# Gated cross-attention and a two-expert feed-forward: the sorted rows packed without a gap

## The reference

```
x = x + tanh(g_xattn) * attention(layernorm(x), ctx)      # 16 heads of 16, 77 keys, softmax, output projection
n = layernorm(x)                                          # 2048 rows of 256
top1 = argmax(n @ gate_w.T)                               # expert 0 or 1 for each row
masked[e] = n where top1 == e, else 0
routed = sum over e of relu(masked[e] @ w1[e] + b1[e]) @ w2[e] + b2[e]      # hidden 1024
shared = relu(n @ sw1 + sb1) @ sw2 + sb2
x = x + tanh(g_ffn) * (routed + shared)
```

## Time and profile before

| | us |
|---|---|
| median of 3 runs (lowest, highest) | 352.51 (351.61, 352.97) |
| the profiled execution | 354.73 |
| its span | 353.0 |
| PE busy in the span | 323.2 (92%) |
| DVE busy | 223.5 (63%) |
| ACT busy | 217.3 (62%) |
| POOL busy | 197.1 (56%) |

### The profile page before, as it was taken

How to read it: one execution, slowest core, us unless ns; L and a number is a source line. 1 busy time by engine, 2 the same in 40 slices (tenths; PEclk the granted TensorE clock), 3 DMA queues, 4 the chain that set the end, 5 groups by cost and what they waited for, 6 DMA issues and landing times.

```text
span 353.0 us, 7375 instructions
## 1 busy us (share of the span) xinstructions
PE 323.2 (92%) x2407; PEld 288.8 (82%) x2407; DVE 223.5 (63%) x490; ACT 217.3 (62%) x491; POOL 197.1 (56%) x274
## 2 busy tenths in 40 slices
PE   7984769889999999999999989999999999999970
PEld 6662658667989778797889969999999999999970
DVE  6999578999889657668957925334354435343540
ACT  3565586976785866847948553546655656464640
POOL 7467578673765478537480785244553544464432
PEclk9999588999999999999999999999999999999996
DMA  6999695280515241203330210212311321022110
GB/s 193 293 308 240 107 315 146 71 212 4 143 34 120 43 92 58 72 3 120 121 119 2 68 53 30 88 34 63 89 60 30 89 78 37 25 71 88 49 41 30
DMA packets 40230, 33.88 MB, mean 96 GB/s; under 512 B 16697, under 2 KB 37709, under 8 KB 40205
## 3 DMA queue, kind: packets, MB, share of 16 engines
q1 hardware_dynamic: 36552, 25.80, 27.2%
q0 software_dynamic: 2816, 7.09, 6.3%
q10 hardware_dynamic: 837, 0.67, 0.7%
HBM read 21.72 MB, written 12.35 MB: 97 GB/s over the span
## 4 chain that ended last, share of the span: by engine, by line
PE 67%; DVE 10%; DMA 6%; POOL 5%; SPq 4%; issue 3%; ACT 1%; another core or an unknown queue 1%; ACTq 0%; POOLq 0%; DVEq 0%
PE y_ps L1405 23%; PE h_ps L1405 16%; PE s_ps L1405 11%; PE bank L1405 10%; DMA x_all<-in_x 5%; PE bank L1538 4%; SPq L516 1%; DVE smax L1173 1%; POOL sorted_dram L667 1%; PE bank L1642 1%; DVE rsum L1191 1%; SPq L458 1%; DMA k_own<-k_dram 1%; POOL hT_lo L676 1%; POOL nt L692 1%
## 5 line engine op out<-in xcount | busy, mean ns | idle before, releaser
L1371 DVE TENSOR_TENSOR hT_lo<-h,hT_hi 128x256 fp32r<-128x256 f32 x72 | 32.5, 452 | 45.2 <-ACT h L1027 42.1
L648 POOL TENSOR_TENSOR probs<-probs,rinv 128x616 f32<-128x616 f32 x32 | 41.4, 1293 | 27.6 <-DVE rinv L1195 27.5
L1024 ACT ACTIVATE hT_hi<-h_ps,vec_cols 128x256 fp32r<-128x256 f32 x36 | 17.1, 475 | 43.3 <-PE h_ps L1405 39.9
L1405 PE MATMUL y_ps<-ew_hi,hT_hi 128*128 128x256 f32 x144 | 41.5, 288 | 0.0
L1405 PE MATMUL y_ps<-ew_hi,hT_lo 128*128 128x256 f32 x144 | 40.3, 280 | 0.0
L1405 PE MATMUL y_ps<-ew_lo,hT_hi 128*128 128x256 f32 x144 | 40.3, 280 | 0.0
L937 ACT ACTIVATE hT_hi<-h_ps,vec_cols 128x512 fp32r<-128x512 f32 (+1 forms) x40 | 24.7, 617 | 24.8 <-PE h_ps L1405 24.4
L1405 PE MATMUL y_ps<-sw_hi,hT_hi 128*128 128x256 f32 x128 | 38.1, 297 | 1.8 <-POOL hT_lo L676 1.7
L777 POOL DMA_INDIRECT out<-final,scatter_token x18 | 19.6, 1092 | 29.9 <-issue 16.2
L1405 PE MATMUL y_ps<-sw_lo,hT_hi 128*128 128x256 f32 x128 | 36.1, 282 | 0.0
L1405 PE MATMUL y_ps<-sw_hi,hT_lo 128*128 128x256 f32 x128 | 36.1, 282 | 0.0
(11 more groups left out here) (197 smaller groups left out, 1054.8 us busy)
## 6 DMA issues: line engine op xcount, KB each, us to landing
v_diag<-v_rows SPq DMA_DIRECT2D x16, 256.0 KB
stage<-in_L_ffn_w SPq DMA_DIRECT2D x4, 1024.0 KB, 5.4
sorted_dram<-empty_rows SPq DMA_DIRECT2D x10, 257.0 KB, 8.9
xs<-sorted_dram SPq DMA_DIRECT2D x10, 257.0 KB
stage<-in_L_ffn_sw SPq DMA_DIRECT2D x2, 1024.0 KB, 7.1
x_all<-in_x SPq DMA_DIRECT2D x1, 1536.0 KB, 10.3
part_dram<-x_all SPq DMA_DIRECT2D x3, 512.0 KB
k_dram<-probs SPq DMA_DIRECT2D x2, 616.0 KB, 10.2
```

Source lines behind the costliest of these rows:

```text
L648: nc.gpsimd.tensor_tensor(pq, pq, rinv[:, b % 2, k, :].unsqueeze(2).to_broadcast([P, HG, KEYS]), ALU.mult).then_inc(p_ready, 1)
L1024: nc.scalar.activation(hT[0][:, c % HB, 0:RTOK], hidden_bank(c % 4)[:, 0:RTOK], ACT.Relu, bias=b1_sb[:, 1 + e, c:c + 1]).then_inc(h_hi, 1)
L1371: nc.vector.tensor_tensor(hT[1][:, c % HB, 0:RTOK], h32[:, c % 2, 0:RTOK], hT[0][:, c % HB, 0:RTOK], ALU.subtract).then_inc(h_lo, 1)
L1405: return nc.tensor.matmul(out_, lhsT, rhs, start=start, stop=stop, **kw)
```

## The change

The rows are packed without a gap: rows of expert 0 from the front, rows of expert 1 from the back of exactly 2048 slots. The tile in the middle then has rows of both. It is run with one expert only, the one that has the middle of the tile, and the half of it (128 rows) in which the seam lies is run again at the end with the other expert, and only the rows of that expert are written. So there are 8 rounds (9 if one expert has at most 128 rows) and a half tile.

- One fill DMA is left, of the 256 slots behind the end.
- `seam` computes five numbers (`plan`) in seven more small DVE operations, and three for the rows to be dropped.
- Into the place of the shared weights, ACT copies the weights of the half tile's expert by four DMAs of 1 MB each from SBUF to SBUF, after its waits for the last shared product and all expert weights and before its first routed evacuation.
- The half tile: first layer of 8 x 2 x 3 products with 128 columns, second layer of 8 x 3 products with 256 columns; evacuations and splits of 128 columns; one gather, one add, one final of 256 columns and one scatter.
- All five orders are new. POOL splits chunks 1, 4 and 5 of a unit instead of 1, 3, 4, 5 and 6; ten quarters are folded instead of eleven.

```diff
-RTILES = TOKENS // RTOK + 1
-SLOTS = RTILES * RTOK
+RTILES = TOKENS // RTOK
+MOST_ROUNDS = RTILES + 1
-LO_ON_POOL = (1, 3, 4, 5, 6)
-FOLDED = {2, 4, 11, 12, 16, 19, 22, 23, 26, 28, 31}
+LO_ON_POOL = (1, 4, 5)
+FOLDED = {2, 4, 11, 12, 16, 19, 25, 29, 30, 31}
...
 PE_ORDER = """
-    warm.0 yt.0 yt.1 yt.2 yt.3 vt warm.1 kp.0.0 kp.0.1 in.0.0 kp.1.0 kp.1.1 qy.0.1 vp.0 in.1.0 vp.1 vp.2 qy.1.1
-    sc.0.0 sc.0.1 vp.3 sc.0.2 sc.0.3 sc.1.0 sc.1.1 in.2.0 tn.0.0.1 tn.0.1.1 qy.2.0 sc.1.2 sc.1.3 tn.0.2.1
+    warm.0 yt.0 yt.1 yt.2 yt.3 vt warm.1 kp.0.0 in.0.0 kp.0.1 kp.1.0 qy.0.1 kp.1.1 sc.0.0 vp.0 in.1.0 vp.1 vp.2
+    qy.1.1 vp.3 sc.0.1 sc.0.2 sc.0.3 sc.1.0 sc.1.1 tn.0.0.0 tn.0.1.1 in.2.0 qy.2.1 sc.1.2 sc.1.3 tn.0.2.0
...
-    di.7.3 hl.19 hl.20 ro.3.0 ro.3.1 hl.21 ro.3.2 ro.3.3 hl.22 ro.4.0 ro.4.1 scat.3 hl.25 ro.4.2 ro.4.3 hl.27
-    hl.28 hl.29 scat.4 hl.30 hl.33 hl.35 hl.36 hl.37 hl.38
+    ro.2.0 ro.2.1 ro.2.2 ro.2.3 di.6.2 scat.1 di.6.3 di.7.0 scat.2 hl.17 di.7.1 di.7.2 di.7.3 hl.20 hl.21 ro.3.0
+    ro.3.1 ro.3.2 ro.3.3 hl.25 ro.4.0 ro.4.1 hl.28 ro.4.2 hl.29 ro.4.3 scat.3 scat.4 hl.33 hl.36 hl.37
...
 SP_ORDER = """
-    fl.0 fl.1 kw.0 vz.0 vz.1 kw.1 fl.2 fl.3 kr.1 kr.2 vw.0 fl.4 vw.1 wd.0 wd.1 vr.0 kr.3 vw.2 vr.1 wd.3 kr.4
-    vr.2 vw.3 wd.2 vw.4 kr.5 vr.3 vr.4 vw.5 kr.6 vr.5 vw.6 ps.0 vw.7 kr.7 vr.6 vr.7 ps.1 wd.4 wd.5 ps.2 xs ps.3
-    ps.4
+    fl.0 kw.0 vz.0 vz.1 kw.1 kr.1 kr.2 wd.0 vw.0 wd.1 vw.1 vr.0 kr.3 vw.2 vr.1 vr.2 kr.4 vw.3 wd.3 vw.4 vr.3
+    kr.5 vr.4 wd.2 vw.5 vw.6 vr.5 kr.6 vw.7 ps.0 kr.7 vr.6 vr.7 ps.1 wd.4 wd.5 ps.2 ps.3 xs ps.4
 """
...
@@ SP
+            def fill():
 
                 sp.wait_ge(empty_made, 2)
+                rows = sorted_dram[TOKENS:TOKENS + RTOK, :].rearrange("(t p) d -> p t d", p=P)
+                sp.dma_start(rows, empty_rows[:, :, :]).then_inc(filled, 16)
...
+            with sp.Fori(0, rounds - 1) as j:
                 sp.wait_ge(xsT_ps, j + 1)
                 sp.wait_ge(ids_copied, j + 1)
+                load_sorted(j + 1 - again)
+            sp.wait_ge(xsT_ps, rounds)
+            sp.wait_ge(ids_copied, rounds)
+            sp.dma_start(xs[:, 0, :], sorted_dram[bass.ds(shared_half * P, P), :]).then_inc(xs_in, 16)
...
@@ POOL
+            pool.wait_ge(half_ids, 1)
+            pool.indirect_dma_start(
+                out=half_part[:, :], out_offset=None, in_=part_dram[:, :],
+                in_offset=bass.IndirectOffsetOnAxis(ap=half_token[:, 0:1], axis=0),
+                bounds_check=last_token, oob_is_err=False).then_inc(half_gathered, 16)
+            pool.wait_ge(half_gathered, 16)
+            pool.wait_ge(half_in, 16 * 2)
+            nc.gpsimd.tensor_tensor(half_part[:, :], half_part[:, :], half_other[:, :], ALU.add).then_inc(half_added, 1)
+            pool.wait_ge(half_ids, 2)
+            pool.wait_ge(half_done, 1)
+            pool.indirect_dma_start(
+                out=out[:, :], out_offset=bass.IndirectOffsetOnAxis(ap=half_token[:, 1:2], axis=0),
+                in_=half_final[:, :], in_offset=None, bounds_check=last_token, oob_is_err=False).then_inc(half_out, 16)
...
@@ ACT
+            act.wait_ge(y_used, CHUNKS_SHARED)
+            for n in range(2, 6):
+                act.wait_ge(w_lo[n], 1)
+            for n in range(2):
+                act.dma_start(sw1_sb[n][:, :, :].rearrange("p k h -> p (k h)").bitcast(F32),
+                              ew[:, bass.ds(half_expert, 1), n, :].rearrange("p o h -> p (o h)").bitcast(F32)
+                              ).then_inc(half_w, 16)
+                act.dma_start(sw2_sb[n][:, :, :].rearrange("p k d -> p (k d)").bitcast(F32),
+                              ew[:, bass.ds(half_expert, 1), 2 + n, :].rearrange("p o h -> p (o h)").bitcast(F32)
+                              ).then_inc(half_w, 16)
...
@@ PE
+            pe.wait_ge(xsT_lo, rounds + 1)
+            pe.wait_ge(half_w, 16 * 4)
+            for n in range(HC + 3):
+                if n < HC:
...
+                    for kc in range(KC):
+                        ins = cut(hidden_bank(n % 4)[:, 0:P], lambda m: sw1_sb[m][:, kc, n * P:(n + 1) * P],
+                                  lambda m: xsT[m][:, bass.ds(rounds % 2, 1), kc, 0:P].rearrange("p o s -> p (o s)"),
+                                  kc == 0, kc == KC - 1)
+                    ins.then_inc(half_h, 1)
+                if n >= 3:
+                    c = n - 3
+                    pe.wait_ge(half_lo, c + 1)
+                    if c == 0:
+                        pe.wait_ge(final_rdy, rounds)
+                    ins = cut(y_ps[:, 0, :], lambda m: hT[m][:, c % HB, 0:P], lambda m: sw2_sb[m][:, c, :], c == 0,
+                              c == HC - 1, skip_group_check=True)
+                    ins.then_inc(half_y, 1)
```

More of the change, by code:

```diff
@@ L96 @@
[L96 to L105, removed]
@@ L1034, in routed @@
                         sorted_hi(j + 1, SORTED_BANK)
-            with act.Fori(0, tiles_of_0) as j:
+            with act.Fori(0, first) as j:
                 routed(j, 0)
-            with act.Fori(tiles_of_0, RTILES) as j:
+            with act.Fori(first, rounds) as j:
                 routed(j, 1)
+            act.wait_ge(half_in, 16 * 2)
+            for c in range(HC):
+                act.wait_ge(half_h, c + 1)
+                if c < HB:
+                    act.wait_ge(y_used, rounds * HC + CHUNKS_SHARED)
+                else:
+                    act.wait_ge(half_y, c - HB + 1)
+                nc.scalar.activation(hT[0][:, c % HB, 0:P], hidden_bank(c % 4)[:, 0:P],
+                                     ACT.Relu, bias=half_b1[:, c:c + 1])
+                if c >= 2:
+                    act.wait_ge(half_lo, c - 1)
+                else:
+                    act.wait_ge(h_lo, rounds * HC + LO_DVE)
+                nc.scalar.activation(h32[:, c % 2, 0:P], hidden_bank(c % 4)[:, 0:P], ACT.Relu, bias=half_b1[:, c:c + 1]
+                                     ).then_inc(half_32, 1)
         @block.vector
@@ L1394, in routed, with half_hidden_lo @@
                 ).then_inc(final_rdy, 1)
-            with dve.Fori(0, tiles_of_0) as j:
+            with dve.Fori(0, first) as j:
                 routed(j, 0)
-            with dve.Fori(tiles_of_0, RTILES) as j:
+            with dve.Fori(first, rounds) as j:
                 routed(j, 1)
+            def half_hidden_lo(c):
+                dve.wait_ge(half_32, c + 1)
+                nc.vector.tensor_tensor(hT[1][:, c % HB, 0:P], h32[:, c % 2, 0:P], hT[0][:, c % HB, 0:P],
+                                        ALU.subtract).then_inc(half_lo, 1)
+            dve.wait_ge(xs_in, rounds * 16 + 16)
+            nc.vector.tensor_copy(half_token[:, 0:1], xs[:, 0, DIM:ROW]).then_inc(half_ids, 1)
+            dve.wait_ge(seam_step, SEAM_OPS + 4)
+            nc.vector.tensor_tensor(half_token[:, 1:2], xs[:, 0, DIM:ROW], half_drop[:, :], ALU.add).then_inc(half_ids, 1)
+            for c in range(HC):
+                half_hidden_lo(c)
+            dve.wait_ge(half_y, HC)
+            dve.wait_ge(half_added, 1)
+            dve.wait_ge(rows_out, rounds * 32)
+            nc.vector.scalar_tensor_tensor(out=half_final[:, :], in0=y_ps[:, 0, :], scalar=gains[:, 1:2],
+                                           in1=half_part[:, :], op0=ALU.mult, op1=ALU.add).then_inc(half_done, 1)
         @block.tensor
```

236 lines of the change are left out of this document (148 added, 88 removed).

## The result

The changed kernel takes **349.68 us** (median of nine runs, 347.41 to 351.52) against 351.61 for the kernel before on the same chip: a ratio of 0.992 [0.990, 0.995]. In a second set it took 349.12 against 352.73, 0.990 [0.987, 0.993]. So it is faster by 0.8 to 1.0%, where 2.4% were forecast (343.9). The profiled execution took 349.01, span 347.3; that of before 354.73, span 353.0. Terms are compared by profile first and then by medians. Launches over 1.5% above the fastest of their kernel count as slow: so did three of the twelve of the second set, the profiled one among them (the median of the other nine is 348.53), and the profiled one of the last experiment.

A forecast was written before the change was run, and what follows sets the result against it. It took matmul count and pitch to bound the routed stage, and PE's feeders the first 80 us. Terms -7 - 3.7 - 1.1 + 0.7 + 2.5 = -8.6 gave 346.1 profiled, 343.9 us median, range 337 to 351.5.

The forecast's parts named there:

- before the routed stage: First 80 us and on to the routed stage: fewer fills and new orders save 7 us, bounds 0 and -14.
- nine rounds to eight and a half: Routed stage: a round of 11.8 us becomes a half tile of 8.1, products at 0.11 each: -3.7 us.
- the end: After the last matmuls: one scatter less and narrower final and split, against a slightly late addend: -1.1 us.
- The copy of the weights: Start of the routed stage: four 1 MB DMAs from ACT cost +0.7 us for issues and +2.5 for bytes.
- The issues, +0.7: ACT before its first routed evacuation: four issues take 1.7 us, delaying PE by 0.7; bounds 0 and +5.
- The bytes, +2.5: First routed round: 4.2 MB delay the next sorted rows, landing 2.3 us late; +2.5 taken, bounds 0 and +10.
- Rival C: Routed stage start: copy holds ACT as DMAs drain, +22, 363 us; decided where issues exceed 12 us; chance 0.07.
- the -4: Before the routed stage: without fills, key loads start 2.0 to 5.5 us earlier; PE's wait of 5.0 shrinks to 1.
- the +1: Before the routed stage: ten splits move to DVE, some four before 120 us where it is nearly full: +1 us.
- rival B: Half tile: fp32r at 128 columns takes two passes, 0.245 us a product, +6.5; 350.0 us; chance 0.15.
- Rivals D: Before the routed stage: the new order closes nearly every wait, -14 us there; 336.9 us; chance 0.11.
- E: Before the routed stage: gain at the keys given back at DVE and ACT by 100 us, 0 there; 350.9; chance 0.12.

The follow-up runs named there:

- the last experiment: The changed kernel with the half tile's 48 first-layer matmuls 64 columns wide instead of 128: 354.65 us profiled and 348.07 us, two runs.

## Why the prediction was wrong

By its own terms, in us; "medians" are worked out from the experiments (no copy: 341.35 - 352.73 = -11.4 for the first three together, less the rounds' and the end's profile values; the copy: 349.12 - 341.35):

| step | forecast | profiles | medians |
|---|---|---|---|
| before the routed stage | -7 | -9.2 | -5.7 |
| nine rounds to eight and a half | -3.7 | -3.9 | |
| the end | -1.1 | -1.8 | |
| the copy (0.7 + 2.5) | +3.2 | +9.2 | +7.8 |
| sum | -8.6 | -5.7 | -3.6 |

The copy's 9.2 is that of one profile; in the three others that have it as in the changed kernel the first round is 11.4, 7.9 (fills back) and 10.3 (64 columns) above the later ones.

**The step that failed is "The copy of the weights".** It was put at 3.2 and cost 7.8. Its two ways, the hold of ACT and the lateness of the rows, were right, and both sizes were too small; it missed that the first feeds the second, and the clock. It missed in three places.
- *The issues, +0.7.* SP's 0.37 to 0.48 per MB was taken for each of the four. Measured: 0.56, 0.53, 1.31, 1.26, 4.0 from the first start to the last end. PE waited 3.0; with 4 KB each it still waited 1.5. The row for the upper bound, 1.35 a fill under load, was in hand and was the one that applied to the last two. Rival C had the mechanism (later DMAs are held while earlier ones drain) but not the size, and its deciding point of 12 us was not reached.
- *The bytes, +2.5.* The estimate had the rows land 5.0 after the issue and 2.3 late. They took 7.8 and were 2.8 late, from an issue that the hold of ACT had put off, by way of DVE: 6.9 into the round (226.39 to 233.31), before only 2.6 (235.60 to 238.23). The two costs are not independent, as the sum has them. The gathers, which I let "fit into the same stall", are a stall of their own once that one is taken away: 2.9 in the kernel with SP's issue.
- *The clock, counted at nothing.* The sum charged slow clock to the stall on the keys but none to the stalls that the copy makes. It is 3.4 of the 9.2 here.

The Trainium skill (DMA: Bandwidth & Descriptors, Queues, rings and completion order) has an engine drain a whole packet, typically 9 to 17 descriptors, from one queue row before it turns to the next; the forecast took the turn to be a single piece of 8 KB. The 7.8 measured lies above the 5.0 of that reading; no run here shows the length of a turn, so whether that is the reason stays open.

**Before the routed stage** the profile gave 9.2 for 7, and the medians about 5.7; the forecast lies between. Against the median start of the seven profiles with this prelude, 227.3, the profile of before gives 8.3, and less the 3.1 by which that profile lies above its own median it is 5.2. The fills carry it: with them back all of it is gone (first routed product 236.24). That it goes by way of the keys, as the -4 has it, is shown only in part: taking the wait on the keys away in the old order brought about 2, and with the fills back in the new order that wait was only 1.9, while a late load of weights cost 3.0. The size of the sum is in part luck. The wait of 1.7 on POOL is gone as forecast; the +1 is in no run by itself. The clock is no fixed gain: with the same program and waits the same to 0.3 it was 1.00 and 1.00, or 0.91 and 0.91.

**The half tile** was right: one pass at a pitch of 0.11, 8.6 against 8.1 forecast (the last drain included), and rival B is out. The term is -3.9, not 8.6 - 11.8 = -3.2, because the rounds after the first took 11.77 where the nine before took 11.85 each; what made them 0.08 shorter is not shown. **The end** gave 1.8 for 1.1: POOL's add waited on nothing new; its gather landed in time and the 0.5 put down for it was not lost.

Rivals D (336.9) and E (350.9) were ways for the prelude to go. E's number is near the result, for a reason that is not E's. The signs set out: the stage started before 233 (226.39), the wait on the keys is gone, the clock is over 0.9, one scatter is left, the half tile is as said. "The first round longer by 2" and "issues under 0.5 each" failed. The 5.8 idle us of the first round came just under the 6 named as the mark of failure; in the second profile of the same kernel they are 7.5.

## What to carry to other kernels

A bulk copy of data that is needed late is priced by what else is in flight when it starts. Cut it into pieces of a size that the slack of each round covers, and issue them behind the small transfers of the round, from an engine on which nothing waits; here that turned 7.8 us into nothing that the medians show, and made 341.5 of 349.1. When a change adds a wait of about 3 us to a PE that never idled, add the matmuls that follow at half the clock to its price: 3.4 us after two waits here, where a wait of 1.5 was followed by none. And fills or other loads that nothing needs soon are priced by all that the same queue issues behind them, not by the one wait that the profile names: with the fills back it was another one.

## What the runs showed of the hardware

- Of four 1 MB copies SBUF to SBUF in a row the third and fourth took 1.3 us to issue on ACT, 1.37 and 1.62 on SP, the first two 0.5 to 0.6; with 4 KB each all four took 0.53 to 0.57. ACT's next instruction started only behind the fourth (230.97).
- While they ran at 379 to 424 GB/s, PE worked at full rate (4.00 of 4.00 at 1.00 in one window of 234 to 238 with SP's issue), but a 257 KB load took 7.8 us to land (8.0 to 9.5 in three other profiles) against a median of 3.0.
- Products of fp32r with 128 moving columns have a pitch of 0.11, with 64 columns the same, with 256 0.118. In the one profile with 64 columns the granted clock fell to 1.2 GHz without a wait of PE in the half tile; in the seven with 128 it did not.
- The granted clock differs between launches of one program: 1.00 and 1.00 in 20 to 60 us in one profile, 0.91 and 0.91 in another, with PE's waits the same to 0.3 us.
